# Second stage of a graph network kernel: row gathers held behind steps of VectorE instead of TensorE's sums

## The reference

```
# stage 1: x1 = layernorm(x + L0(x)), per edge also relu(edge_attr @ ee_w1 + b)
# stage 2, per node:
h   = (1 + eps) * x1 + segment_sum(x1[src] + e, dst)
h   = relu(ln(h @ w1 + b1))          # 256 -> 1024
h   = relu(ln(h @ w2 + b2))          # 1024 -> 1024
y   = h @ w3 + b3                    # 1024 -> 256
out = layernorm(x1 + relu(ln(x1 + y)))
```

## Time and profile before

| | us |
|---|---|
| median of 3 runs | 1134.37 |
| lowest, highest | 1134.0, 1136.73 |
| span of the profiled execution | 1477.5 |

### The profile page before, as it was taken

The page is one execution under the profiler, slowest core; times in us unless marked ns, Lnnn a source line. Parts: engine busy times, 40 slices in busy tenths (PEclk is TensorE's granted clock), DMA queues, the critical chain, the costliest instruction groups (busy, mean ns, idle before and its releaser), DMA issues.

```text
span 1477.5 us, 21215 instructions
## 1 busy us (share of the span) xinstructions
PE 1201.4 (81%) x5297; PEld 977.9 (66%) x5297; DVE 976.8 (66%) x2795; ACT 686.1 (46%) x1677; POOL 812.9 (55%) x840
## 2 busy tenths in 40 slices
PE   4788877787777887778777889888898898898897
PEld 3576666566666665566555677677776777776676
DVE  4767755667656775667666666666666676676575
ACT  2455644556445554455453443443533443443444
POOL 7555555455554555545645565566565566566530
PEclk9798887888878888788878899999999999999999
DMA  6345544445444444435565555656665566566540
GB/s 202 105 120 145 151 130 144 125 142 147 134 143 128 128 127 119 126 114 148 146 203 163 165 169 172 185 167 183 176 185 166 174 176 178 171 185 180 161 119 13
DMA packets 106088, 222.13 MB, mean 150 GB/s; under 512 B 20003, under 2 KB 57369, under 8 KB 106010
## 3 DMA queue, kind: packets, MB, share of 16 engines
q0 software_dynamic: 53408, 164.16, 39.1%
q1 hardware_dynamic: 52602, 57.11, 12.4%
HBM read 203.96 MB, written 17.23 MB: 150 GB/s over the span
## 4 chain that ended last, share of the span: by engine, by line
PE 34%; another core or an unknown queue 21%; DVE 16%; issue 16%; ACT 11%; DVEq 1%; DMA 1%; POOL 1%; ACTq 0%; POOLq 0%
PE ps_z L1386 8%; PE ps_e L1108 7%; PE ps_sum L1115 3%; PE ps_sum L1113 3%; ACT msg L1658 3%; ACT aF L1888 3%; PE ps_y L1386 3%; PE ps_s L1330 3%; DVE msg L2162 2%; DVE oh L216 2%; PE ps_tr L1455 2%; DVE msg L2168 2%; PE ps_w L1209 2%; ACT msg L1661 2%
## 5 line engine op out<-in xcount | busy, mean ns | idle before, releaser
L970 POOL DMA_INDIRECT raw<-in_x,src_all x399 | 385.6, 966 | 321.9 <-DVE msg L2168 177.2
L1031 POOL DMA_INDIRECT grow<-table_dram,src_all x401 | 392.7, 979 | 275.0 <-issue 115.1
L1108 PE MATMUL ps_e<-we,attr 65*128 65x256 f32 x832 | 251.1, 427 | 150.7 <-DVE msg L2168 127.0
L2162 DVE SCALAR_TENSOR_TENSOR msg<-raw,w_sb,msg 128x256 fp32r<-128x256 f32 x416 | 183.0, 478 | 242.5 <-issue 130.5
L1108 PEld LDWEIGHTS ps_e<-we,attr 65*128 65x128 f32 x832 | 171.5, 214 | 200.4 <-issue 173.3
L1661 ACT ACTIVATE msg<-ps_e 128x512 fp32r<-128x512 f32 (+1 forms) x220 | 124.3, 565 | 310.2 <-remote 221.1
L1113 PE MATMUL ps_sum<-msg,oh 128*128 128x512 f32 x464 | 255.8, 551 | 9.2 <-DVE msg L2168 8.8
L1386 PE MATMUL ps_z<-w_high,a 128*128 128x512 f32 x784 | 255.5, 395 | 7.7 <-issue 6.3
L216 DVE TENSOR_SCALAR oh<-lane,rel 128x128 fp32r<-128x128 f32 x871 | 208.1, 297 | 18.9 <-issue 15.7
L1115 PE MATMUL ps_sum<-msg,oh 128*128 128x512 f32 x464 | 210.1, 453 | 0.0
L1658 ACT ACTIVATE msg<-raw,w_sb 128x256 fp32r<-128x256 f32 x416 | 188.1, 498 | 10.3 <-issue 7.7
(11 more groups left out here) (189 smaller groups left out, 1591.6 us busy)
## 6 DMA issues: line engine op xcount, KB each, us to landing
attr<-in_attrT SPq DMA_DIRECT2D x50, 192.0 KB
raw<-in_x,src_all POOLq DMA_INDIRECT x416
grow<-table_dram,src_all POOLq DMA_INDIRECT x401
w_raw<-in_m_w SPq DMA_DIRECT2D x48, 128.0 KB
table_dram<-table SPq DMA_DIRECT2D x23, 256.0 KB
attr<-in_attrT SPq DMA_DIRECT2D x24, 160.0 KB
xs<-in_x SPq DMA_DIRECT2D x24, 128.0 KB
xTb<-in_xT SPq DMA_DIRECT2D x24, 128.0 KB
```

The lines of the kernel that those rows point to most:

```text
L970: pool.indirect_dma_start(out=raw[:, j, :], out_offset=None, in_=x, in_offset=bass.IndirectOffsetOnAxis(ap=src_all[:, q * TILES + j:q * TI ...
L1031: pool.indirect_dma_start(out=grow[:, j, :].bitcast(F32), out_offset=None, in_=table_dram, in_offset=bass.IndirectOffsetOnAxis(ap=src_all[ ...
L1108: mm = pe.matmul(ps_e[k % 3][:, (j - j0) * D:(j - j0 + 1) * D], attr[:, j * P:(j + 1) * P], we1[:, :], start=True, stop=True)
L2162: dve.scalar_tensor_tensor(msg[:, j, 1, 0:D], raw[:, j, :], w_sb[:, tile_cols(n, j)], msg[:, j, 0, 0:D].bitcast(F32), ALU.mult, ALU.subtract)
```

## The change

The two holds of `row_gather` for positions 3 to 24 go. In their place the first gather of each pair, k = j // 2 = 1 to 8, waits for a step of VectorE's iteration (`follow`). The wait for `row_free` stays as it was. Tiles 0 and 1 have no hold.

```diff
-            FEW_AHEAD, MORE_AHEAD = 4, 13
...
+                def follow(p, k):
+
+                    if k == 1:
+                        pool.wait_ge(a_ready[1], 2 * (p - 3) + 1)
+                    elif k == 2:
+                        pool.wait_ge(a_ready[1], 2 * (p - 3) + 2)
+                    elif k == 3:
+                        pool.wait_ge(a_ready[0], 2 * (p - 2) + 2)
+                    elif k == 4:
+                        pool.wait_ge(h_ready, p)
+                    elif k == 5:
+                        pool.wait_ge(hT_ready, p)
+                    elif k == 6:
+                        pool.wait_ge(fin, FIN * (p - 3) + 9)
+                    elif k == 7:
+                        pool.wait_ge(zn_ready[1][1], p - 1)
+                    else:
+                        pool.wait_ge(ln[0], LN * (p - 1) + 3)
+                    pool.nop(nofuse=True)
+
                 def row_gather(path, p, b, j):
 
                     free = path.row_free(p, j // 2)
-                    if WINDOWS < p < BLOCKS and j >= FEW_AHEAD:
-                        free = max(free, SUMS * p)
                     if free > 0:
                         pool.wait_ge(sum_done, free)
                         pool.nop(nofuse=True)
-                    if WINDOWS < p < BLOCKS and j >= MORE_AHEAD:
-                        pool.wait_ge(h_turned, p)
-                        pool.nop(nofuse=True)
+                    if WINDOWS < p < BLOCKS and j % 2 == 0 and j > 0:
+                        follow(p, j // 2)
                     pool.indirect_dma_start(
```

## The result

The changed kernel takes 1241.1 us (1239.29 to 1243.51, 4 runs) against 1134.35 us before: ratio 1.0931, 95% interval 1.0912 to 1.095. It is 107 us slower, 4.85 us for each of the 22 positions. Forecast were +33 us and a range that ended at 1203. The sign and the place were right, the size was not.

What follows compares the result with a forecast made beforehand. TensorE was taken to bound the kernel, busy 570 of 660 us of stage 2. A 1.5 us wait in each of 22 positions gave +33 us on 1134.4, so 1167 us; range 1132 to 1203.

Steps and rivals of the forecast that it cites:

- The late releases: Stage 2 semaphore waits, such as ScalarE's 4.85 us, 20 times; assumed to belong mostly to the profiled execution.
- faster, 1107: Rival: gather bursts cause the late releases; spreading them removes VectorE's 27.5 us of waits, about 1107 us; chance 0.10.
- The last sign: Profile of the changed kernel: prediction is wrong if ScalarE's 4.85 us wait for the turned h is gone.
- Removing the holds: GpSimd's old holds for the sums and turned h: nothing waits for these gathers, so TensorE gains zero.
- Pairs 1 to 6 at nothing: Gathers of tiles 2 to 13: their new waits end before the tiles are wanted, so they cost nothing.
- Pairs 7 and 8: Tiles 14 to 16: queue behind tile 14's zn wait makes tile 16 late, 1.5 us in each of 22 positions.
- The size of the lateness: Tile 16 at TensorE's last sum: 1.9 us in the profile, 1.4 outside it, 1.5 taken; bounds 0.3 to 3.5.
- The lead of zn over TensorE: Outside the profile, zn is ready some 0.6 us before TensorE is through with layer 1.
- The next position's tile 0: Gather queued behind tile 16: the next position's tiles 0 to 3 were mentioned, but no cost was given for them.
- The slow clock: Rival: TensorE's new idle time lowers its granted clock, 1.6 us more per position, 1202 us in all; chance 0.10.
- The forecast case: One tile late by 0.4 to 2.8 us in each position, 1143 to 1195 us; chance 0.70.
- the upper landing bound: Gather start to use at most 5.1 us, making tile 16 up to 3.5 us late per position, 1211 us.

Runs made afterwards that it cites:

- b_again: The kernel before the change, unchanged, profiled a second time: 1135.96 us, profile span 1134.1 us.
- free: The kernel with neither the old holds nor the new waits; gathers wait only for their free part of the buffer: 1132.12 us, ratio 0.9964.
- k7_only: The changed kernel with one wait alone, tile 14's gather for VectorE's zn step, and no old holds: 1241.22 us, ratio 1.0926.
- a_fill: The changed kernel with ten more matmuls in each iteration, placed where TensorE stood before tiles 14, 15 and 16: 1210.23 us, ratio 1.0664.
- k3_only: The changed kernel with one wait alone, tile 6's gather for the second split of layer 1, no old holds: 1156.83 us, ratio 1.0183.

## Why the prediction was right or wrong

**What bounds the kernel.** Right: TensorE, 95% busy in `b_again`, and 2.2 us of waits for a gather in 520 us there. Wrong was what I said of GpSimd. I gave it 20% of free time; 17 issues of 1.25 us against an iteration of 22.4 us leave it 1.2 us. I had both numbers, 21.3 us of issues and a TensorE bound near the median, and read GpSimd's time off the stretched profile.

**The late releases.** Right to set them aside: `b_again` has none, and the rival "faster, 1107" fell with them. `free` holds gathers least of all and takes 1132 us: no run lost time to bursts. The last sign that the prediction gave for being wrong, that ScalarE's wait of 4.85 us for the turned h is gone, came true (11.2 us in 22 waits in the changed kernel), but it tells nothing, since the wait is gone from `b_again` too.

**Removing the holds is worth nothing.** Right within 0.4% (`free`).

**Pairs 1 to 6 at nothing.** Wrong, the second step that failed. Pairs 3 and 5 cost 21 and 62 us when alone. I compared each tile with its own time of use and forgot my own sentence that behind a waiting gather stand later gathers. For pair 5 that would have given tile 16, with the prediction's own terms, 1029.22 + 0.2 + 7.5 + 3.0 = 1039.9, 0.9 us late by the time of use in that profile (1039.02) and not nothing. In the changed kernel this cost is hidden behind pair 7's, so it did not move the sum.

**Pairs 7 and 8.** Right in mechanism, as far as it went, and in which decides: pair 7 through the queue, `k7_only` = 1241. The event, the transposes that start beside it, the two gathers in front and the gap before `ps_y` are all in the profile after.

**The size of the lateness**, the first step that failed: 1.5 us forecast, 2.87 measured. Two terms were too small. From VectorE's end to the issue I took 0.2 us, which no row gave; it is 0.77 (906.91 to 907.68). For issue to use I took 3.0 us between 1.9 and 5.1; it is 3.91. The profile gives for the 336 gathers between 640 and 1180 us of the changed kernel

```profile
DMA to landing us min/median/max: 3.2/3.7/5.0
```

These two make 0.57 + 0.91 = 1.48 us, and with the 1.4 us that the prediction had worked out before it rounded up they give 2.88. The lead of zn over TensorE that I worked out as 0.6 us was right: 907.60 - 906.91 = 0.69. The Trainium skill's fit for such a DMA (DMA: Bandwidth & Descriptors, Anatomy of one DMA), 2.6 us, lies below the shortest landing here; the measurement decides.

**The next position's tile 0**, the third step that failed: it was put at nothing without a reason. The prediction counted the next position's tiles 0 to 3 in the queue behind tile 16 and stopped its sum at tile 16. Tile 0 is wanted 0.59 us behind tile 16 and issued 1.25 us behind it, and costs 0.57 us more in the iteration shown, 22 x 0.57 = 13 us.

**The slow clock**, the fourth. I had it as a rival at 1.6 us a position and a chance of 0.10, as something that either comes or doesn't. It came in the iteration shown, 1.53 us behind tile 0, and `a_fill` prices it at 31 us over the kernel. Lateness 2.87, tile 0 0.57 and clock 1.53 make 4.97 us, and 22 x 4.97 = 109 us, the whole result. The forecast case and this rival were not two cases: the mean granted clock falls from 0.995 to 0.962 as the reckoned lateness grows from 0.5 to 2.85 us. The range ended at 1203 because I let the upper landing bound and the clock stand as alternatives. Together, 22 x (3.5 + 1.6), they reach 1247 us. That this bound lies near the 1241 measured is in part luck, since tile 0 is not in it.

Still open is why four waits cost 4 us more than the worst of them.

## What to carry to other kernels

Judge a hold in a queue by the items behind it that are wanted first: the end of the step waited for, the start-up, the issue time of everything in front, and the landing, against the time of use. Go on past the item that seems the last: here the next position's first tile stood behind it and was later still. The largest of such delays counts, and they don't add. A queue that is itself near the period (21.3 us of issues in 22.4) has little to catch up with. By the 3.9 us from issue to use, tile 16 had some 1.4 us in hand in `b_again` and tile 0 some 0.7, and a stop is paid at the tail once that is used up. And a long wait on TensorE is to be priced with the slow clock behind it, not beside it.

## What the runs showed of the hardware

- A gather of 128 rows of 2 KB takes 3.2 to 5.0 us from issue to landing, 3.7 in the median, at a DMA share of 0.62 (640 to 1180 us of the changed kernel), and GpSimd issues one every 1.25 us.
- GpSimd starts a gather 0.77 to 0.78 us after the end of the VectorE instruction that releases it, with a no-op between the wait and the gather (zn, hT and split steps of the changed kernel).
- After a broken stretch (gaps of 0.35, 0.84 and 1.00 us within 3 us) TensorE's granted clock was 0.73 over the next 6.3 us, which holds stretches at each of its two levels; matmuls of 256 columns started 0.21 us apart in place of 0.12. Ten matmuls in the gaps kept it at 0.996 over the kernel and made the kernel faster with more work in it. Stands of 0.30 and 0.23 us in an iteration of `k3_only` left it at 1.00.

```profile
915.97 0.63 PE L1402 MATMUL ps_y<-w_high,a 128*128 128x256 f32 x2
916.40 0.41 PE L1402 MATMUL ps_y<-w_low,a 128*128 128x256 f32 x1
...
919.24 0.40 PE L1402 MATMUL ps_y<-w_high,a 128*128 128x256 f32 x2
919.48 0.28 PE L1402 MATMUL ps_y<-w_low,a 128*128 128x256 f32 x1
```

The rows are of the changed kernel. The first two are at the half clock; the last two, 3 us later, are at the full one.
- One profile of a kernel can be 30% longer than its runs, with semaphore releases late by 4 to 5 us at the same place in each iteration, while the next profile of the same kernel is not. The busy time of VectorE and ScalarE held (977 and 686 us against 986 and 687); the waits did not, nor did TensorE's (1201 us at a mean granted clock of 0.891, against 1080 at 0.994).
